# Four-gather groups that wait for each other, and two thirds of a residual sum added inside the next layer

## The reference

```python
x = L0_attn_x
xn = _layernorm(x, axis=-1)
x = x + _L0_attn_ref(xn, ...) + _L0_ffn_ref(xn, ...)
xn = _layernorm(x, axis=-1)
x = x + _L1_attn_ref(xn, ...) + _L1_ffn_ref(xn, ...)
...
```

```python
def _L0_ffn_ref(x, wg, w1, w3, w2):
    NUM_EXPERTS = 8
    CAPACITY = 512
    bz, slen, dim = x.shape
    xt = x.reshape(bz * slen, dim)
    scores = jax.nn.softmax(xt @ wg, axis=-1)
    top_scores, sel = jax.lax.top_k(scores.T, CAPACITY)
    token_idx = sel.reshape(-1)
    routed = xt[token_idx] * top_scores.reshape(-1, 1)
    routed = routed.reshape(NUM_EXPERTS, CAPACITY, dim)
    h = jax.nn.silu(jnp.einsum('ecd,edh->ech', routed, w1)) * jnp.einsum('ecd,edh->ech', routed, w3)
    routed_out = jnp.einsum('ech,ehd->ecd', h, w2).reshape(-1, dim)
    out = jnp.zeros_like(xt).at[token_idx].add(routed_out)
    return out.reshape(bz, slen, dim)
```

## Time and profile before

| | |
|---|---|
| median of three runs | 2309.42 us |
| the profiled execution, its time | 2311.24 us |
| its span, first to last instruction | 2309.4 us |
| PE busy | 2110.0 us, 91% |
| DVE busy | 1467.4 us, 64% |
| ACT busy | 1125.3 us, 49% |
| POOL busy | 896.0 us, 39% |
| DMA moved | 36.89 MB |

### The profile page before, as it was taken

How to read it: one execution, slowest core, us unless ns; L and a number is a source line. 1 busy time by engine, 2 the same in 40 slices (tenths; PEclk the granted TensorE clock), 3 DMA queues, 4 the chain that set the end, 5 groups by cost and what they waited for, 6 DMA issues and landing times.

```text
span 2309.4 us, 48271 instructions
## 1 busy us (share of the span) xinstructions
PE 2110.0 (91%) x16216; PEld 1573.4 (68%) x16216; DVE 1467.4 (64%) x4253; ACT 1125.3 (49%) x3600; POOL 896.0 (39%) x1416
## 2 busy tenths in 40 slices
PE   5887977399999999999999999999979999999998
PEld 2565644277777777777777666666657777777776
DVE  6999834365665666665666655555556777777775
ACT  3443342154454444444444355554545655665654
POOL 3113245344444444444444311111114544544544
PEclk9877779599999999999999899999999999999999
DMA  6000016600000000000000000000000000000001
GB/s 193 2 1 1 12 30 158 168 1 2 2 2 1 2 2 2 1 2 1 2 1 2 1 0 0 0 0 0 0 0 2 2 2 2 2 2 2 2 2 37
DMA packets 37478, 36.89 MB, mean 16 GB/s; under 512 B 5648, under 2 KB 34448, under 8 KB 36368
## 3 DMA queue, kind: packets, MB, share of 16 engines
q1 hardware_dynamic: 31632, 29.82, 4.1%
q0 software_dynamic: 5632, 4.33, 1.3%
HBM read 23.53 MB, written 10.62 MB: 15 GB/s over the span
## 4 chain that ended last, share of the span: by engine, by line
PE 68%; DVE 5%; ACT 4%; issue 3%; POOL 1%; DMA 1%; DVEq 0%; POOLq 0%; SPq 0%; ACTq 0%
PE bank L1314 8%; PE bank L1303 6%; PE bank L1240 5%; PE bank L1289 5%; PE bank L1286 5%; PE bank L1336 4%; PE bank L1283 3%; PE bank L1225 3%; PE bank L1227 2%; PE bank L1226 2%; PE bank L1306 2%; PE bank L1701 2%; PE bank L1723 2%; PE bank L1233 2%; PE bank L1725 2%
## 5 line engine op out<-in xcount | busy, mean ns | idle before, releaser
L1597 POOL TENSOR_TENSOR work<-work 128x128 f32<-128x128 f32 (+1 forms) x1048 | 503.3, 511 | 743.3 <-DVE work L1497 743.3
L1375 ACT ACTIVATE work<-bank,work 128x128 f32<-128x128 f32 x524 | 191.8, 366 | 624.0 <-DVE work L1486 624.0
L1492 DVE COPY work<-bank 128x384 f32<-128x384 f32 x520 | 281.9, 547 | 32.2 <-PE bank L1314 4.2
L1376 ACT ACTIVATE work<-bank,work 128x256 f32<-128x256 f32 x524 | 247.2, 472 | 0.0
L1314 PE MATMUL bank<-w_const,work 128*128 128x128 f32 x1560 | 228.2, 282 | 0.4 <-POOL work L1597 0.4
L1485 DVE TENSOR_REDUCE work<-bank 128x1 f32<-128x128 f32 x524 | 149.5, 285 | 110.4 <-PE bank L1289 102.9
L1486 DVE TENSOR_REDUCE work<-bank 128x1 f32<-128x256 f32 x524 | 216.6, 413 | 0.0
L1518 DVE COPY work<-bank 128x512 f32<-128x512 f32 x136 | 94.0, 691 | 166.2 <-PE bank L1235 159.6
L1314 PEld LDWEIGHTS bank<-w_const,work 128*128 128x128 f32 x1560 | 166.2, 141 | 45.8 <-issue 39.2
L1303 PE MATMUL bank<-work 128*64 128x256 f32 x1032 | 169.0, 405 | 0.3 <-DVE work L1518 0.3
L1394 ACT ACTIVATE work<-bank 128x512 f32<-128x512 f32 x266 | 162.3, 610 | 8.7 <-PE bank L1227 8.5
(11 more groups left out here) (338 smaller groups left out, 4989.7 us busy)
## 6 DMA issues: line engine op xcount, KB each, us to landing
w_l<-in_l SPq DMA_DIRECT2D x1, 3210.5 KB, 10.6
w_l<-in_l SPq DMA_DIRECT2D x2, 1540.0 KB
w_f<-in_f SPq DMA_DIRECT2D x1, 3072.0 KB, 13.9
x_sb<-in_x SPq DMA_DIRECT2D x4, 512.0 KB, 5.9
normed_rows<-work SPq DMA_DIRECT2D x1, 2048.0 KB, 9.3
even_experts<-x_sb SPq DMA_DIRECT2D x8, 256.0 KB, 3.6
residual<-x_sb SPq DMA_DIRECT2D x1, 2048.0 KB, 9.6
qk<-in_qk SPq DMA_DIRECT2D x2, 1024.0 KB
```

The costliest lines, as they stand in the source:

```text
L1376: act.activation(pr[g % 4][:, Q1], scored(i, g)[:, Q1], ACT.Exp, bias=nmx[:, g % 4, 1:2], accum_out=sm[:, g % 4, 1:2]).then_inc(s_ex.s, 1)
L1492: dve.tensor_copy(pt[g % 4], PS[2 + g % 2][:, 0:384]).then_inc(s_te.s, 1)
L1597: ins = pool.tensor_tensor(w, w, spread(rc[:, g % 4, q:q + 1], w.shape[1]), ALU.mult)
```

## The change

1. In `gathered`, every group but the first waits until the group just ahead of it has landed.
2. `acc_back` becomes three pieces of 9, 9 and 14 tiles (`ACC_TILES`), each at its own place in `work`: columns 6144, 1812 and 4096 on. The last two lie in the areas of layer 1's two value buffers.
3. SP brings `acc_d` back in three DMAs, and x in three parts of the same sizes. Ahead of the first it also waits for `b_y` = 8, the copy of the last expert's output.
4. DVE's adds move to a function, `experts_added(dve, c)`. Layer 0 calls it for piece 0 alone. Layer 1 calls it for pieces 1 and 2, right after `rest(0)`, and waits there until all three adds are done.

```diff
             def gathered(e):
-                if e >= 3:
-                    pool.wait_ge(b_got[e % 3], 16 * CT * (e // 3))
+                if e >= 1:
+                    pool.wait_ge(b_got[(e - 1) % 3], 16 * CT * ((e + 2) // 3))
...
-        acc_back = xg_cols[:, 0:TILES * D]
+        ACC_TILES = ((0, 9), (9, 18), (18, TILES))
+        acc_back = [work[:, at:at + (b - a) * D].rearrange("p (t d) -> p t d", d=D) for at, (a, b) in zip((6144, 1812, 4096), ACC_TILES)]
...
-        x_back = [sem(f"x_back{c}") for c in range(4)]
+        x_back = [sem(f"x_back{c}") for c in range(len(ACC_TILES))]
...
-            dve.wait_ge(acc_in, 16)
-            for c in range(4):
-                dve.wait_ge(x_back[c], 16)
-                dve.tensor_tensor(x_sb[:, 8 * c:8 * c + 8, :], x_sb[:, 8 * c:8 * c + 8, :],
-                                  acc_back[:, 1024 * c:1024 * c + 1024].rearrange("p (t d) -> p t d", d=D), ALU.add).then_inc(x_sum, 1)
-            dve.wait_ge(x_sum, 4)
+            experts_added(dve, 0)
+            dve.wait_ge(x_sum, 1)
+
+        def experts_added(dve, c):
+            a, b = ACC_TILES[c]
+            dve.wait_ge(acc_in, 16 * len(ACC_TILES))
+            dve.wait_ge(x_back[c], 16)
+            dve.tensor_tensor(x_sb[:, a:b, :], x_sb[:, a:b, :], acc_back[c], ALU.add).then_inc(x_sum, 1)
...
             sp.wait_ge(b_xs, E0)
+            sp.wait_ge(b_y, E0)
             sp.wait_ge(b_added[0], 16 * CT * E0 // 2)
-            sp.dma_start(acc_back.rearrange("p (t d) -> p t d", d=D), acc_v).then_inc(acc_in, 16)
+            for c, (a, b) in enumerate(ACC_TILES):
+                sp.dma_start(acc_back[c], acc_v[:, a:b, :]).then_inc(acc_in, 16)
             sp.wait_ge(b_added[1], 16 * CT * E0 // 2)
             sp.wait_ge(b_acc, 16)
-            for c in range(4):
-                sp.dma_start(x_sb[:, 8 * c:8 * c + 8, :], res_v[:, 8 * c:8 * c + 8, :]).then_inc(x_back[c], 16)
+            for c, (a, b) in enumerate(ACC_TILES):
+                sp.dma_start(x_sb[:, a:b, :], res_v[:, a:b, :]).then_inc(x_back[c], 16)
...
                 dve.wait_ge(*taken0)
                 rest(0)
+                if moe:
+                    for c in range(1, len(ACC_TILES)):
+                        experts_added(dve, c)
+                    dve.wait_ge(x_sum, len(ACC_TILES))
```

## The result

The kernel after took **2288.39 us** (median of 4 runs, 2285.65 to 2292.35); the kernel before, beside it, 2308.26 (4 runs, 2306.66 to 2311.13): a ratio of **0.9914** (0.9895 to 0.9933), 20 us faster. I had forecast 2302.5 within 2294.5 to 2308.8: the direction was right, the size and the range were wrong. A second result came late: in two of the eight comparisons of this study the kernel before itself took 2288 us, and in the one of them that had the kernel after beside it the same change was worth nothing that can be told, 0.9991 (0.998 to 1.0003). I call the other six comparisons, where before took 2307 us or more, the high condition and these two the low one. Both results have to be explained. The profiled execution after took 2289.51 us, span 2287.7 us, 21.7 less than before.

A forecast was written before the change was run, and what follows sets the result against it. TensorE, busy 91% of the span, was taken as the bound, so only its standstill could be won. Opening -4.85, readback 0 and gather waits -2 gave -6.9 us: 2302.5 us from the median 2309.42, range 2294.5 to 2308.8.

The forecast's parts named there:

- Opening: Between layers 0 and 1: the close needs only 9 of 32 tiles, so layer 1 starts 4.85 us earlier.
- the 0.62 us of cover: Layer 1's opening: the moved adds end at 445.23, 0.62 us before the copy of the values is due at 445.85.
- Readback in three pieces at 0: End of layer 0: fetching the even experts' sums in three transfers changes nothing, taken as 0 within -3.2 to +4.8 us.
- Rival 2: The opening's gain is eaten by the three-piece readback or late adds: 2309.4, or 2306 to 2308; chance 0.22.
- I take -2: Layer 0's last four attention steps: the gather waits were taken to win 2 us.
- my bound of -11: Gather stage: most the waits could win, up to 8 us of unexplained gaps plus 3.4 us of clock.
- Rival 1: Runs of gathers were the whole trouble; gaps go and the clock stays up: -4.85 - 9 gives 2295.5; chance 0.18.
- the run of twelve: Twelve gathers on POOL with hardly a gap, 308.9 to 324.2 us, beside about 8 us of unexplained gaps at most.
- two sets of matmuls: PE's 32 small matmuls, twice a step, take 3.64 us at 1.2 GHz against 1.93: 3.4 us for both sets.
- The waits themselves cost 0: POOL, gather stage: delays of 1.4 to 2.3 us per group stay hidden behind existing idle time, costing 0.
- Rival 3: Slower: waits put groups 5 and 6 onto the last two heads' transposes and 32 small matmuls: +6.5, 2316; chance 0.08.
- Rival 4: The gather waits do nothing, groups having landed already: -4.85 alone, 2304.6; chance 0.52 together with the forecast.

The follow-up runs named there:

- acc_only: The kernel before with only the second part, readback in three pieces and two adds in layer 1's opening, old gather waits: 2304.25 us, ratio 0.9983.
- acc_again: The second part alone on the kernel before, gather waits as before, measured again in another comparison: 2304.01 us, ratio 0.9983.
- g_only: The kernel before with only the new gather waits, each group waiting for the one ahead; adds as before: 2292.80 us, ratio 0.9935.
- g_space2: The kernel before, old gather waits, with two dead 128x512 products on POOL ahead of groups 1, 3, 5 and 6: 2299.33 us, ratio 0.9958.
- after_again: The kernel after unchanged, measured once more, beside a kernel before at 2287.45 us: 2287.42 us, ratio 0.9991.
- g_56: The kernel before with the new landing wait for gather groups 5 and 6 alone: 2305.38 us, ratio 0.9975.
- first4: The kernel after with the three pieces at 4, 14 and 14 tiles instead of 9, 9 and 14: 2287.05 us, ratio 0.9911.
- later: The kernel after with the gather groups moved behind the key blocks (0 | 1 2 | 3 4 | 5 6 7): 2292.43 us, ratio 0.9926.
- g_breath: The kernel before with one dead 128x1 product on POOL ahead of groups 1, 3, 5 and 6: 2288.41 us, ratio 0.9998 beside before at 2288.06.

## Why the prediction was wrong

- **Opening: right.** -4.96 for -4.85; by the medians of acc_only and acc_again -4.0 and -4.4. The copy of the values was late by 0.05 us. I had named a copy released by VectorE's own adds as a sign of being wrong, and the profile does put it down to them: the 0.62 us of cover were too small to keep PE the releaser, but nothing was lost by it.
- **Readback in three pieces at 0: right**, 6.69 us in both, although it went in 4092 packets instead of 1040. That the two are equal to the digit is luck: over the other profiles it is 6.0 to 6.9 us in one piece and 6.0 to 7.0 in three. The rule that a DMA engine switches only at packet boundaries (the Trainium skill, "DMA: Bandwidth & Descriptors", section "SWDGE vs HWDGE vs iDMA") would have won up to 3.2 us if the profile's packets are the page's: the trace doesn't bear it out here. The fixed 2.0 us of its section "Anatomy of one DMA — SWDGE (gpsimd) path" is fitted on DMAs that GpSimd issues; for these, which SP issues, 4 us more for two more DMAs were not paid. Rival 2 falls with it.
- **"I take -2" for the gather waits: this step failed.** They gave -12.1 us in the profile and -15.4 in g_only's median, beyond even my bound of -11. Rival 1 named the mechanism and priced it at -9. Even rival 1's 2295.5 was 7 us short. I erred in three places. (a) I took the earlier trace rows for the whole trouble, the run of twelve. The eight gathers of groups 0 and 1, 0.30 us apart, had a stall as well, ACT's 2.23 us "remote" at 287.73 printed above, and I hadn't read that row. The "two runs of four from 291.6 to 302.2" that I set against it, which have 1.19 us between them, do show nothing "remote"; but the granted clock was 0.50 from 290 to 299 while they ran, behind the stall ahead of them. (b) I priced the clock for two sets of matmuls (3.4 us), not for the stage. (c) I let "the same gathers fall on the same steps" weigh as an argument against; g_space2 shows that the same gathers with 2.2 us of room four times do much less harm (stage 72.8).
- **"The waits themselves cost 0": true only where the stalls are.** The cover I used, POOL waiting 2.79 and 4.01 us for ACT's keys, was itself made by stalls upstream. Without them POOL is due there at once, as the row of after_again at 288.02 shows, and the waits cost some 3 us. A wait was also longer than I said: 2.3 us between issues, where I had at most 1.7.
- **Rival 3** didn't come at its price, but what it describes exists: in g_56 group 6 falls on the heads of the step before the last, which reach VectorE 3.7 us late; in first4 and later it is the last ones, 1.8 and 2.8. Rival 4 (2304.6) is refuted by g_only, but is the nearest one to the low condition: there the waits win nothing that shows, and cost some 3 us besides.
- **Not foreseeable from the profile**: that before has a second level 20 us lower. One profile shows one of them.

**What is shown and what isn't.** Shown: in the high condition the 32 indirect gathers, issued as before, cost 12 to 20 us of the stage (83 to 86 us against 65.5 to 71.2 with waits, pauses or plain DMAs in their place; 72.8 and 73.5 in g_space2 and later); landing waits and pauses take most of that away, not all; the second part is worth 4 to 5 us. Not shown: how a gather holds back the other engines' releases; that there is a length of run below which it does no harm (four behind a landing wait still did); whether the rate or an instruction between them decides; what makes the low condition; that before has no stalls in it (argued from g_breath's equal time and its 63.5 us of stage); the second part's worth alone there.

## What to carry to other kernels

When one engine issues many indirect DMAs in a row and others show idle time "remote" or a low granted clock beside them, put a cheap instruction or a landing wait between them and look again; here a pause of 0.3 us between single gathers did at least as well as a wait of 2.3 us between groups (stage 67.7 against 69.3 to 71.2, one profile each). Don't take the slack behind a stalled step as cover: it goes with the stall. Compare a kernel with its forerunner more than once at different times before trusting a gain of 1%: here the same pair gave 0.9914 and 0.9991.

## What the runs showed of the hardware

- In the high condition, 32 indirect gathers of 128 rows, 1.24 us apart, coincide with completions of PE that reach ACT and DVE late: 1.55 us behind the end of PE's record at 287.73 and 3.4 at 320.99 in before, 3.7 in g_56. The scatters, 1.87 us apart, and plain DMAs of the same bytes, 0.54 us apart, do not.
- With 1.47 us between their starts no wait is put down to "remote" (one profile, and four runs at 2281.26 to 2286.43).
- The kernel before has two levels that go with the comparison: medians of 2307.5 to 2313.2 us in six, 2287.5 and 2288.1 in two.
- A first part of 4 tiles of x is added 3.07 us after its issue (414.52 - 411.45; 2.85 to 3.07 in four profiles), one of 9 tiles 4.27 (up to 4.54) and one of 8 tiles 4.14 us (4.08 to 4.34).
